# Attention with one exponential per key tile for both heads, scores issued ahead of the value matmuls, and a second input buffer in the first LayerNorm stage

## The chip, the cores and the metric

The kernel runs on the eight NeuronCores of one Trainium2 chip. Each core gets 4 of the 32 sequences of 2048 rows and 1024 features and runs the same program on them; the cores exchange nothing. The time is device microseconds (us) of the slowest core. Each core has TensorE (PE, with its weight loads shown apart as PEld), VectorE (DVE), ScalarE (ACT), GpSimd (POOL) and SyncE (SP); every engine works through its own instructions in order and waits on semaphores. On-chip memory is SBUF; matmul results land in PSUM.

## The reference

```python
xn = layernorm(x)                       # over the 1024 features, eps 1e-5
x  = x + attn(xn) + ffn(xn)
# attn: 16 heads. q1, q2, k1, k2 = xn @ W (4 numbers per head each)
L_q = exterior(q1, q2); L_k = exterior(k1, k2)      # 6 numbers, normalised
scores = einsum(L_q, L_k @ J6.T) * 6 ** -0.5        # causal mask, softmax
out = einsum(softmax(scores), xn @ W_v.T + b_v) @ W_out.T + b_out
# ffn: complex linear map with W_real, W_imag (512x512, unfolded from small factors)
out_real = x_real @ W_real.T - x_imag @ W_imag.T + bias_real
out_imag = x_real @ W_imag.T + x_imag @ W_real.T + bias_imag
```

## The kernel before

A core works on its 4 images one after another. For each image there are these stages:

- `A1_tile` (lines 270 to 297): for one of 16 row tiles (128 rows x 1024) SP loads x into `xst`; DVE squares it into `x2st`, sums both and works out mean and variance; ACT makes the reciprocal deviation by Ln and Exp (lines 287, 289); DVE writes the normalised tile to `xnst` (line 294). `A2_tile` transposes it on PE (line 307) through the two PSUM banks F6 and F7 into `xnT`.
- `B1_chunk` and `B2_chunk` project q and k and build the six numbers per head; `V_group` (line 401) makes the values, kept in `vaug` with a column of ones for each head, so that row 64 of the product is the softmax denominator; `FFN_pass1` does the complex map and writes y.
- Attention: for each of 4 groups `g` of four heads, `C_scatter` spreads the six numbers of the heads over partitions (32 a head), then 8 calls of `C_pair`: `pr` (which 2 of the 4 heads) times `w` (which 512 queries). All heads' outputs go to `oT`; `burst_outproj` multiplies by `W_out` and adds to y by DMA.

`C_pair(b, g, pr, w)` is where most of the time goes, with 128 calls in a run. It walks over `nkt = 4 * w + 4` key tiles `kt` of 128 keys; there are 1280 such steps in a run. The last four steps of a call lie on the causal diagonal; they work on 512, 384, 256 and 128 queries and need a triangular mask on their first 128. The other steps work on all 512. For head j of 2, a step has a score matmul (S, line 557, only 6 rows deep; the two heads use different row groups of the array), an exponential on ACT (line 578) from PSUM `S` to `exps`, on the diagonal a mask on DVE (line 583), and a value matmul (AV, line 591) that adds into `O4`. `S` and `exps` have two slots, used by even and odd `kt`. S runs two steps ahead: `emit_scores(0)` and `emit_scores(1)` stand at the start, `emit_scores(kt + 2)` behind the AV matmuls of `kt`.

The division by the softmax sum is put off: `emit_divide` of one call (lines 610 to 639) is issued in the next, after its first two S steps. ACT takes Ln and Exp of the sum row (lines 618, 620), SP sends the result to DRAM (625) and reads it back to 64 partitions (630), and DVE multiplies (636) from `O4` to `oT`. Since there is a single `O4`, the first AV of the next call waits until that is done (`o4_free`).

Work of the next image's stages is woven into attention: `pace()` at the end of each step issues items of two queues (`A1_tile`, `A2_tile`, `FFN_pass1`, and from the fourth group on `B1_chunk`, `B2_chunk`, `V_group`). In the last image there is none of it. In the first image stages A, B, V and FFN come ahead of attention with nothing beside them; its A stage also has the 16 steps that unfold the FFN weights, two behind each of tiles 0 to 7.

Below, AV(k), S(k), exp(k) and mask(k) are those of step `kt` = k of a call, and n is its number of steps. A pair is one call of `C_pair`.

Of the kernel before, what the change touches and what calls it, by code (L numbers as in the profile page):

```python
# [9 lines left out]
F32 = mybir.dt.float32  # L10
BF16 = mybir.dt.bfloat16
AF = mybir.ActivationFunctionType
OP = mybir.AluOpType
AX = mybir.AxisListType
# [74 lines left out]
def mkap(sl, extra_offset, free_dims, nparts=None):  # L89
    p = list(sl.ap[0])  # L90
    if nparts is not None:
        p[1] = nparts
    return AP(sl.tensor, sl.offset + extra_offset, [p] + [list(d) for d in free_dims])


def pi_out_ap(tens):
    return mkap(tens, 0, [[512, 2], [1, 32], [32, 16]])


def build(nb=NB, debug=False):  # L100
# [4 lines left out]
    x_d = din("x", [nb, T, D])  # L105
# [23 lines left out]
    with st:  # L129
# [12 lines left out]
        tri_sb = sb("tri", [128, 128], BF16)  # L142
# [12 lines left out]
        exp_sb = sb("exps", [128, 2048], BF16)  # L155
        xstage = sb("xst", [128, 1024], F32)
# [14 lines left out]
        for name in ["dwp", "dxp", "dws", "dyt", "dx", "dx2", "dyp", "dya", "dbo", "dbi", "dtr", "t", "v", "s"]:  # L171
# [6 lines left out]
        TE, VE, SE, GE, SY = nc.tensor, nc.vector, nc.scalar, nc.gpsimd, nc.sync  # L178

        stx = {  # L180
            "xst_r": 0,
            "x2_r": 0,
            "xn_r": 0,
            "f_w": [0, 0],
# [82 lines left out]
        unf_steps = deque([(lambda ri=ri, mt=mt: unf_step(ri, mt))  # L267
                           for ri in range(2) for mt in range(8)] + [unf_fin])

        def A1_tile(b1, tt):  # L270
            vS.wait(SY, stx["xst_r"])
            dx.inc(SY.dma_start(xstage[:], x_d[b1, tt * 128:(tt + 1) * 128, :]), 16)
            dx.wait(VE)
            dx2.wait(VE)
            vS.inc(VE.tensor_tensor(x2stage[:], xstage[:], xstage[:], OP.mult))
            vS.inc(VE.reduce_sum(stat[:, 0:1], xstage[:], axis=AX.X))
            vS.wait(VE)
            vS.inc(VE.reduce_sum(stat[:, 1:2], x2stage[:], axis=AX.X))
            stx["x2_r"] = vS.n
            vS.inc(VE.tensor_scalar(stat[:, 2:3], stat[:, 0:1], 1.0 / 1024, None, OP.mult))  # L280
            vS.wait(VE)
            vS.inc(VE.tensor_scalar(stat[:, 3:4], stat[:, 1:2], 1.0 / 1024, None, OP.mult))
            vS.inc(VE.tensor_tensor(stat[:, 4:5], stat[:, 2:3], stat[:, 2:3], OP.mult))
            vS.wait(VE)
            var_s = vS.inc(VE.tensor_tensor(stat[:, 5:6], stat[:, 3:4], stat[:, 4:5], OP.subtract))  # L285
            vS.wait(SE, var_s)
            sS.inc(SE.activation(stat[:, 6:7], stat[:, 5:6], AF.Ln, bias=cvec[:, 0:1]))  # L287
            sS.wait(SE)
            rstd_s = sS.inc(SE.activation(stat[:, 7:8], stat[:, 6:7], AF.Exp, scale=cvec[:, 2:3]))
            sS.wait(VE, rstd_s)  # L290
            vS.wait(VE)
            tS.wait(VE, stx.get("xn_r", 0))
            dx2.wait(VE)
            xn_s = vS.inc(VE.tensor_scalar(pi_out_ap(xnstage[:]), xstage[:], stat[:, 2:3],  # L294
                                           stat[:, 7:8], OP.subtract, OP.mult))
            stx["xst_r"] = xn_s
            stx["a_xn"] = xn_s

        def A2_tile(b1, tt):
# [238 lines left out]
                                       S_ps[:, pset * 1024:pset * 1024 + 512]))  # L538

        def C_pair(b, g, pr, w, pace=None):  # L540
            last_kt = 4 * w + 3
            nkt = 4 * w + 4
            exp_snap = {}
# [23 lines left out]
            if stx.get("pending_div") is not None:  # L567
                stx["pending_div"]()
                stx["pending_div"] = None
            avj = {}  # L570
            for kt in range(nkt):
                off = max(kt * 128 - w * 512, 0)
                ss = kt % 2
                for j in range(2):
                    base = ss * 1024 + j * 512 + off
                    end = ss * 1024 + (j + 1) * 512
                    tS.wait(SE, max(avj.get((kt - 2, j), av_snap.get(kt - 2, 0)), sc_snap[kt]))
                    sS.inc(SE.activation(exp_sb[:, base:end], S_ps[:, base:end], AF.Exp))  # L578
                    ej = sS.n
                    if kt >= 4 * w:  # L580
                        sS.wait(VE, ej)
                        in0 = exp_sb[:, base: base + 128]
                        mk = vS.inc(VE.tensor_tensor(in0, in0, tri_sb[:, 0:128], OP.mult))  # L583
                        vS.wait(TE, mk)
                    else:
                        sS.wait(TE, ej)
                    if kt == 0 and j == 0:
                        vS.wait(TE, stx["o4_free"])
                    m4 = 2 * pr + j
                    h = 4 * g + m4  # L590
                    tS.inc(TE.matmul(  # L591
                        O4[:, j * 512 + off:(j + 1) * 512],
                        vaug[:, kt * 1040 + h * 65: kt * 1040 + h * 65 + 65],
                        exp_sb[:, base:end],
                        start=(kt == 0), stop=(kt == last_kt)))
                    avj[(kt, j)] = tS.n
                exp_snap[kt] = sS.n
                av_snap[kt] = tS.n
                if kt + 2 < nkt:
                    emit_scores(kt + 2)  # L600
                if pace is not None:
                    pace()
            stx["av_prev"] = [av_snap[nkt - 2], av_snap[nkt - 1]]
# [39 lines left out]
            stx["pending_div"] = emit_divide  # L643

        for tt in range(NT):
            A1_tile(0, tt)
            A2_tile(0, tt)
            for _ in range(2):
                if unf_steps:
                    unf_steps.popleft()()  # L650
# [94 lines left out]
```

How the kernel before makes its waits and increments, by code:

```python
    def inc(self, instr, k=1):  # L81
        instr.then_inc(self.h, k)
        self.n += k
        return self.n
    def wait(self, eng, n=None):
        eng.wait_ge(self.h, self.n if n is None else n)
```

## Time and profile before

| what | value |
|---|---|
| median of 2 runs | 4822.6 us (4808.25 to 4836.95) |
| the profiled execution | 4833.0 us |
| its span on the slowest core (core 5) | 4831.9 us |
| spans of the eight cores | 4792.6 to 4831.9 us |
| PE busy | 2923.8 us, 61% of the span |
| ACT busy | 1553.7 us, 32% |
| DVE busy | 1447.1 us, 30% |
| first image's stages A, B, V, FFN | 0 to about 560 us |
| attention of the last image | about 4010 to 4720 us |

The busy shares are means over stages of different kinds. The granted clock of PE is a share of 2.4 GHz: 0.50 is 1.2 GHz and 1.00 is 2.4 GHz.

### The profile page before, as it was taken

The numbers are of one execution on the slowest core, as the hardware profiler recorded it, in microseconds if no ns is written. First come the engines' busy times: TensorE is split into PE (matmuls) and PEld (weight loads), VectorE is DVE, ScalarE is ACT, GpSimd is POOL, SyncE is SP. The second block draws the span as 40 slices with busy tenths as digits, with TensorE's granted clock in tenths as the row PEclk, the third lists the DMA queues.
The fourth block names the chain that finished last, engine by engine and source line by source line (L and its number), as shares of the span: only waits on it lengthen the run. The fifth ranks groups of instructions, "written<-read, shape, count | busy, mean of one in ns | idle before, by whom it ended". The sixth has DMA issues, their size and how long they took to land.

```text
span 4831.9 us, 41653 instructions; the slowest of 8 cores (4792.6 to 4831.9 us)
## 1 busy us (share of the span) xinstructions
PE 2923.8 (61%) x10528; PEld 1013.5 (21%) x10528; DVE 1447.1 (30%) x3345; ACT 1553.7 (32%) x3009; POOL 139.4 (3%) x210
## 2 busy tenths in 40 slices
PE   2257555566656755566655865556665586666665
PEld 1114111122112411112211421112221151111112
DVE  4524334332223234332222333433222231111111
ACT  0000244443331044443433014444342204555550
POOL 1200000000000000000000000000000000000001
PEclk9959655566657955556665865556665695555558
DMA  4502201011100410112100041011110032000004
GB/s 107 47 0 70 83 27 33 27 62 61 44 9 7 60 36 27 33 31 66 62 27 11 9 69 33 27 33 48 61 57 7 5 44 35 14 12 12 14 11 72
DMA packets 87180, 180.62 MB, mean 37 GB/s; under 512 B 41760, under 2 KB 42920, under 8 KB 86960
## 3 DMA queue, kind: packets, MB, share of 16 engines
q0 software_dynamic: 56672, 75.38, 8.3%
q1 hardware_dynamic: 30288, 102.58, 7.3%
q8 instruction: 105, 1.72, 0.1%
q14 instruction: 115, 0.94, 0.1%
HBM read 114.36 MB, written 69.73 MB: 38 GB/s over the span
## 4 chain that ended last, share of the span: by engine, by line
PE 46%; DMA 22%; DVE 14%; ACT 10%; issue 8%; DVEq 1%; SPq 0%; ACTq 0%; POOLq 0%; POOL 0%
PE O L591 18%; DMA cdiv<-rscr 10%; PE S L557 8%; DMA y<-ost 8%; PE F L401 5%; PE F L437 3%; DVE oT L636 3%; DMA rscr<-cdiv 3%; ACT cdiv L620 3%; ACT exps L578 3%; ACT cdiv L618 3%; PE F L444 2%; PE F L327 2%; DVE exps L583 1%; PE F L384 1%
## 5 line engine op out<-in xcount | busy, mean ns | idle before, releaser
L578 ACT ACTIVATE exps<-S 128x512 bf16<-128x512 f32 (+3 forms) x2560 | 1199.0, 531 | 2117.9 <-PE S L557 2085.4
L591 PE MATMUL O<-exps,vaug 128*65 128x512 bf16 (+3 forms) x2560 | 1098.0, 511 | 1270.6 <-DVE oT L636 764.3
L591 PEld LDWEIGHTS O<-exps,vaug 128*65 128x65 bf16 x2560 | 281.5, 132 | 1797.2 <-issue 1754.4
L557 PE MATMUL S<-fqp,fkp 6*128 6x512 bf16 (+3 forms) x2560 | 625.1, 501 | 6.2 <-DVE fkp L537 5.5
L636 DVE TENSOR_TENSOR oT<-O,cdiv 64x512 bf16<-64x512 f32 x256 | 174.8, 683 | 905.3 <-DMA cdiv<-rscr 901.2
L583 DVE TENSOR_TENSOR exps<-exps,tri 128x128 bf16<-128x128 bf16 x1024 | 202.6, 225 | 718.5 <-ACT exps L578 712.0
L506 PE MATMUL S<-wout,oT 128*128 128x512 bf16 x1024 | 259.2, 415 | 93.7 <-DVE ost L515 84.2
L557 PEld LDWEIGHTS S<-fqp,fkp 6*128 6x128 bf16 x2560 | 132.8, 97 | 682.1 <-issue 663.1
L401 PE MATMUL F<-wv,xnT 128*128 128x256 bf16 x2048 | 244.2, 276 | 0.6 <-DVE vaug L413 0.5
L307 PE MATMUL F<-idt,xnst 128*128 128x128 f32 x512 | 124.8, 425 | 161.0 <-DVE xnst L294 160.9
L401 PEld LDWEIGHTS F<-wv,xnT 128*128 128x128 bf16 x2048 | 186.5, 98 | 63.4 <-issue 30.4
L377 ACT ACTIVATE scr<-F,cvec 16x512 f32<-16x512 f32 x32 | 21.6, 675 | 491.9 <-PE F L375 491.9
L618 ACT ACTIVATE cdiv<-O 1x1024 f32<-1x1024 f32 x128 | 130.2, 1017 | 128.8 <-PE O L591 128.8
L515 DVE COPY ost<-S 128x1024 f32<-128x1024 f32 x64 | 78.4, 1225 | 293.2 <-DMA y<-ost 250.0
L506 PEld LDWEIGHTS S<-wout,oT 128*128 128x128 bf16 x1024 | 104.3, 105 | 247.0 <-issue 166.3
L620 ACT ACTIVATE cdiv<-cdiv,cvec 1x1024 f32<-1x1024 f32 x128 | 146.8, 1147 | 11.8
L411 DVE TENSOR_TENSOR vaug<-F,bvbc 128x256 bf16<-128x256 f32 x256 | 109.4, 427 | 127.9 <-PE F L401 127.7
L312 DVE CAST xnT<-F 128x512 bf16<-128x512 f32 x128 | 88.6, 692 | 188.3 <-PE F L307 188.3
L452 DVE TENSOR_TENSOR ost<-F,ballbc 128x512 f32<-128x512 f32 x64 | 44.3, 692 | 333.7 <-PE F L437 333.7
L287 ACT ACTIVATE stat<-stat,cvec 128x1 f32<-128x1 f32 x64 | 18.9, 295 | 377.0 <-DVE stat L285 376.7
L307 PEld LDWEIGHTS F<-idt,xnst 128*128 128x128 f32 x512 | 100.4, 223 | 182.2 <-issue 179.8
L437 PE MATMUL F<-wr,xnT 128*128 128x512 bf16 x256 | 100.8, 537 | 48.2 <-DVE negscr L428 48.0
(72 smaller groups left out, 1964.4 us busy)
## 6 DMA issues: line engine op xcount, KB each, us to landing
y<-ost POOLq DMA_DIRECT2D x128, 512.0 KB, 5.3
xst<-x SPq DMA_DIRECT2D x64, 512.0 KB, 4.4
x2st<-x SPq DMA_DIRECT2D x64, 512.0 KB, 4.3
cdiv<-rscr SPq DMA_DIRECT2D x128, 256.0 KB, 3.7
wv<-wvT POOLq DMA_DIRECT2D x8, 256.0 KB, 20.7
wout<-woutT POOLq DMA_DIRECT2D x8, 256.0 KB, 21.5
tascr<-qk POOLq DMA_DIRECT2D x16, 128.0 KB, 2.0
rscr<-cdiv SPq DMA_DIRECT2D x128, 4.0 KB
```

Source lines behind the costliest of these rows:

```text
L307: tS.inc(TE.transpose(Fb[:, c4 * 128:(c4 + 1) * 128], xnstage[:, c * 128:(c + 1) * 128], idt_sb[:]))
L401: ins = TE.matmul(Fb[:, 0:256], xnT[:, kc * 2048 + tt * 128: kc * 2048 + tt * 128 + 128], wv_sb[:, kc * 1024 + g * 256: kc * 1024 + g * 25 ...
L411: vS.inc(VE.tensor_tensor(vaug_ap, Fb[:, 0:256], bvs, OP.add))
L437: ins = TE.matmul(F6[:, 0:512], lhsT, rhs, start=(kc == 0), stop=(kc == 7))
L506: ins = TE.matmul(Pp[:, half * 512:half * 512 + 512], oT[:, pt * 2048 + tt * 128: pt * 2048 + tt * 128 + 128], wout_sb[:, pt * 1024 + half ...
L557: tS.inc(TE.matmul(S_ps[:, ss * 1024 + j * 512 + soff: ss * 1024 + j * 512 + 512], fk_pad[32 * m4:32 * m4 + 6, kt * 128:kt * 128 + 128], f ...
L578: sS.inc(SE.activation(exp_sb[:, base:end], S_ps[:, base:end], AF.Exp))
L583: mk = vS.inc(VE.tensor_tensor(in0, in0, tri_sb[:, 0:128], OP.mult))
L591: tS.inc(TE.matmul(O4[:, j * 512 + off:(j + 1) * 512], vaug[:, kt * 1040 + h * 65: kt * 1040 + h * 65 + 65], exp_sb[:, base:end], start=(k ...
L618: sS.inc(SE.activation(cdiv[32:33, 0:1024], O4[64:65, 0:1024], AF.Ln))
L620: r_s = sS.inc(SE.activation(cdiv[0:1, 0:1024], cdiv[32:33, 0:1024], AF.Exp, scale=cvec[0:1, 3:4]))
L636: vS.inc(VE.tensor_tensor(oT[rr:rr + 64, pt * 2048 + w * 512: pt * 2048 + w * 512 + 512], O4[0:64, j * 512:j * 512 + 512], cdiv[0:64, j * ...
```

## The change

Two edits. In the first image's A stage, odd tiles are loaded into the space of `exps` (not yet in use) with a semaphore of their own, so that two loads can be under way; later images keep one buffer. In `C_pair`, exp and mask of the two heads become one instruction each (of 1024 elements, or 2 x 384, 2 x 256, 2 x 128; the mask of 2 x 128), the AV matmuls of a step come in a row behind them, and `emit_scores(kt + 2)` moves from behind the AV matmuls of `kt` to ahead of them, behind exp(kt). One wait of ACT, on the last use of the `exps` space as input buffer, is added ahead of the first exp.

```diff
--- before.py
+++ after.py
@@ -178,7 +178,7 @@
         TE, VE, SE, GE, SY = nc.tensor, nc.vector, nc.scalar, nc.gpsimd, nc.sync
 
         stx = {
-            "xst_r": 0,
+            "xst_rs": [0, 0],
             "x2_r": 0,
             "xn_r": 0,
             "f_w": [0, 0],
@@ -267,13 +267,16 @@
         unf_steps = deque([(lambda ri=ri, mt=mt: unf_step(ri, mt))
                            for ri in range(2) for mt in range(8)] + [unf_fin])
 
-        def A1_tile(b1, tt):
-            vS.wait(SY, stx["xst_r"])
-            dx.inc(SY.dma_start(xstage[:], x_d[b1, tt * 128:(tt + 1) * 128, :]), 16)
-            dx.wait(VE)
-            dx2.wait(VE)
-            vS.inc(VE.tensor_tensor(x2stage[:], xstage[:], xstage[:], OP.mult))
-            vS.inc(VE.reduce_sum(stat[:, 0:1], xstage[:], axis=AX.X))
+        def A1_tile(b1, tt, slot=0):
+            xs = xstage[:] if slot == 0 else exp_sb[:, 0:2048].bitcast(F32)
+            dxs = dx if slot == 0 else dx2
+            vS.wait(SY, stx["xst_rs"][slot])
+            dxs.inc(SY.dma_start(xs, x_d[b1, tt * 128:(tt + 1) * 128, :]), 16)
+            dxs.wait(VE)
+            if slot == 0:
+                dx2.wait(VE)
+            vS.inc(VE.tensor_tensor(x2stage[:], xs, xs, OP.mult))
+            vS.inc(VE.reduce_sum(stat[:, 0:1], xs, axis=AX.X))
             vS.wait(VE)
             vS.inc(VE.reduce_sum(stat[:, 1:2], x2stage[:], axis=AX.X))
             stx["x2_r"] = vS.n
@@ -291,9 +294,9 @@
             vS.wait(VE)
             tS.wait(VE, stx.get("xn_r", 0))
             dx2.wait(VE)
-            xn_s = vS.inc(VE.tensor_scalar(pi_out_ap(xnstage[:]), xstage[:], stat[:, 2:3],
+            xn_s = vS.inc(VE.tensor_scalar(pi_out_ap(xnstage[:]), xs, stat[:, 2:3],
                                            stat[:, 7:8], OP.subtract, OP.mult))
-            stx["xst_r"] = xn_s
+            stx["xst_rs"][slot] = xn_s
             stx["a_xn"] = xn_s
 
         def A2_tile(b1, tt):
@@ -538,6 +541,9 @@
                                        S_ps[:, pset * 1024:pset * 1024 + 512]))
 
         def C_pair(b, g, pr, w, pace=None):
+            if not stx.get("xbuf_ok"):
+                vS.wait(SE, stx["xst_rs"][1])
+                stx["xbuf_ok"] = True
             last_kt = 4 * w + 3
             nkt = 4 * w + 4
             exp_snap = {}
@@ -567,37 +573,40 @@
             if stx.get("pending_div") is not None:
                 stx["pending_div"]()
                 stx["pending_div"] = None
-            avj = {}
             for kt in range(nkt):
                 off = max(kt * 128 - w * 512, 0)
                 ss = kt % 2
+                tS.wait(SE, max(av_snap[kt - 2], sc_snap[kt]))
+                if off:
+                    e_out = mkap(exp_sb[:], ss * 1024 + off, [[512, 2], [1, 512 - off]])
+                    e_in = mkap(S_ps[:], ss * 1024 + off, [[512, 2], [1, 512 - off]])
+                else:
+                    e_out = exp_sb[:, ss * 1024: ss * 1024 + 1024]
+                    e_in = S_ps[:, ss * 1024: ss * 1024 + 1024]
+                sS.inc(SE.activation(e_out, e_in, AF.Exp))
+                exp_snap[kt] = sS.n
+                if kt + 2 < nkt:
+                    emit_scores(kt + 2)
+                if kt >= 4 * w:
+                    sS.wait(VE, exp_snap[kt])
+                    in0 = mkap(exp_sb[:], ss * 1024 + off, [[512, 2], [1, 128]])
+                    tri_b = mkap(tri_sb[:], 0, [[0, 2], [1, 128]])
+                    mk = vS.inc(VE.tensor_tensor(in0, in0, tri_b, OP.mult))
+                    vS.wait(TE, mk)
+                elif kt + 2 >= nkt:
+                    sS.wait(TE, exp_snap[kt])
+                if kt == 0:
+                    vS.wait(TE, stx["o4_free"])
                 for j in range(2):
-                    base = ss * 1024 + j * 512 + off
-                    end = ss * 1024 + (j + 1) * 512
-                    tS.wait(SE, max(avj.get((kt - 2, j), av_snap.get(kt - 2, 0)), sc_snap[kt]))
-                    sS.inc(SE.activation(exp_sb[:, base:end], S_ps[:, base:end], AF.Exp))
-                    ej = sS.n
-                    if kt >= 4 * w:
-                        sS.wait(VE, ej)
-                        in0 = exp_sb[:, base: base + 128]
-                        mk = vS.inc(VE.tensor_tensor(in0, in0, tri_sb[:, 0:128], OP.mult))
-                        vS.wait(TE, mk)
-                    else:
-                        sS.wait(TE, ej)
-                    if kt == 0 and j == 0:
-                        vS.wait(TE, stx["o4_free"])
                     m4 = 2 * pr + j
                     h = 4 * g + m4
-                    tS.inc(TE.matmul(
+                    ins = TE.matmul(
                         O4[:, j * 512 + off:(j + 1) * 512],
                         vaug[:, kt * 1040 + h * 65: kt * 1040 + h * 65 + 65],
-                        exp_sb[:, base:end],
-                        start=(kt == 0), stop=(kt == last_kt)))
-                    avj[(kt, j)] = tS.n
-                exp_snap[kt] = sS.n
+                        exp_sb[:, ss * 1024 + j * 512 + off: ss * 1024 + (j + 1) * 512],
+                        start=(kt == 0), stop=(kt == last_kt))
+                tS.inc(ins)
                 av_snap[kt] = tS.n
-                if kt + 2 < nkt:
-                    emit_scores(kt + 2)
                 if pace is not None:
                     pace()
             stx["av_prev"] = [av_snap[nkt - 2], av_snap[nkt - 1]]
@@ -643,7 +652,7 @@
             stx["pending_div"] = emit_divide
 
         for tt in range(NT):
-            A1_tile(0, tt)
+            A1_tile(0, tt, tt % 2)
             A2_tile(0, tt)
             for _ in range(2):
                 if unf_steps:
```

On PE, at the start of the very last pair (w = 3 of the last image; the pair before it ends with AV of 128 columns). L557 and L591 are S and AV. Before:

```order
L591 MATMUL O<-exps,vaug 65x128 [waits sem_v] x2
L557 MATMUL S<-fqp,fkp 128x512 [waits sem_s,sem_v]
L557 MATMUL S<-fqp,fkp 128x512
L557 MATMUL S<-fqp,fkp 128x512 [waits sem_s,sem_v]
L557 MATMUL S<-fqp,fkp 128x512
L591 MATMUL O<-exps,vaug 65x512 [waits sem_s,sem_v]
L591 MATMUL O<-exps,vaug 65x512 [waits sem_s]
L557 MATMUL S<-fqp,fkp 128x512 [waits sem_s]
L557 MATMUL S<-fqp,fkp 128x512
L591 MATMUL O<-exps,vaug 65x512 [waits sem_s] x2
```

In the changed kernel, where S is L563 and AV is L603:

```order
L603 MATMUL O<-exps,vaug 65x128 [waits sem_v]
L603 MATMUL O<-exps,vaug 65x128
L563 MATMUL S<-fqp,fkp 128x512 [waits sem_s,sem_v]
L563 MATMUL S<-fqp,fkp 128x512
L563 MATMUL S<-fqp,fkp 128x512 [waits sem_s,sem_v]
L563 MATMUL S<-fqp,fkp 128x512
L563 MATMUL S<-fqp,fkp 128x512 [waits sem_s]
L563 MATMUL S<-fqp,fkp 128x512
L603 MATMUL O<-exps,vaug 65x512 [waits sem_v]
L603 MATMUL O<-exps,vaug 65x512
L563 MATMUL S<-fqp,fkp 128x512 [waits sem_s]
L563 MATMUL S<-fqp,fkp 128x512
```

S(2), which stood behind AV(0), now stands ahead of it, and so ahead of the wait for `o4_free` (sem_v). From then on each S(k+2) waits for exp(k) before AV(k); the AV of undisturbed steps carry no wait of their own.

On PE at the end of the same pair, before:

```order
L557 MATMUL S<-fqp,fkp 128x384 [waits sem_s]
L557 MATMUL S<-fqp,fkp 128x384
L591 MATMUL O<-exps,vaug 65x512 [waits sem_v] x2
L557 MATMUL S<-fqp,fkp 128x256 [waits sem_s]
L557 MATMUL S<-fqp,fkp 128x256
L591 MATMUL O<-exps,vaug 65x384 [waits sem_v] x2
L557 MATMUL S<-fqp,fkp 128x128 [waits sem_s]
L557 MATMUL S<-fqp,fkp 128x128
L591 MATMUL O<-exps,vaug 65x256 [waits sem_v] x2
L591 MATMUL O<-exps,vaug 65x128 [waits sem_v] x2
```

and now:

```order
L563 MATMUL S<-fqp,fkp 128x256 [waits sem_s]
L563 MATMUL S<-fqp,fkp 128x256
L603 MATMUL O<-exps,vaug 65x512 [waits sem_v]
L603 MATMUL O<-exps,vaug 65x512
L563 MATMUL S<-fqp,fkp 128x128 [waits sem_s]
L563 MATMUL S<-fqp,fkp 128x128
L603 MATMUL O<-exps,vaug 65x384 [waits sem_v]
L603 MATMUL O<-exps,vaug 65x384
L603 MATMUL O<-exps,vaug 65x256 [waits sem_v]
L603 MATMUL O<-exps,vaug 65x256
L603 MATMUL O<-exps,vaug 65x128 [waits sem_v]
L603 MATMUL O<-exps,vaug 65x128
```

The last three AV steps now follow each other with only their masks (sem_v) between them.

## Rows read from the trace of the kernel before

**Rows 1.** The page's chain that ended last, by engine.
```profile
PE 46%; DMA 22%; DVE 14%; ACT 10%; issue 8%; DVEq 1%; SPq 0%; ACTq 0%; POOLq 0%; POOL 0%
```
**Rows 2.** Waits of the run: engine line <- releaser: us in total, times, longest.
```profile
DVE oT L636 <- DMA cdiv<-rscr: 901.2, 128, 9.1
PE O L591 <- DVE oT L636: 764.3, 96, 9.1
PE O L591 <- DVE exps L583: 456.2, 238, 9.5
```
**Rows 3.** Timeline, last image, an undisturbed stretch: start us, us, engine, line, operation.
```profile
4142.60 0.61 PE L557 MATMUL S<-fqp,fkp 6*128 6x512 bf16 x2
4143.14 1.06 PE L591 MATMUL O<-exps,vaug 128*65 128x512 bf16 x2
4143.33 1.08 ACT L578 ACTIVATE exps<-S 128x512 bf16<-128x512 f32 x2 [0.45 <-PE S L557]
...
4144.13 0.61 PE L557 MATMUL S<-fqp,fkp 6*128 6x512 bf16 x2
```
**Rows 4.** Windows: PE, PEld, DVE, ACT, POOL busy, PEclk, DMA share, GB/s.
```profile
4144.00:4148.00 4.00, 4.00 (x12) 0.87 (x12) 0.00 (x0) 2.65 (x6) 0.00 (x0) 0.50 0.00 0
...
816.00:818.00 2.00, 1.89 (x10) 0.62 (x8) 0.00 (x0) 2.00 (x5) 0.00 (x0) 1.00 0.00 0
```
**Rows 5.** Timeline, last image: end of one pair, start of the next.
```profile
4152.02 0.85 PE L591 MATMUL O<-exps,vaug 128*65 128x384 bf16 x2
...
4153.07 0.67 PE L591 MATMUL O<-exps,vaug 128*65 128x256 bf16 x2
4153.21 0.45 ACT L578 ACTIVATE exps<-S 128x128 bf16<-128x128 f32 x2 [0.34 <-PE S L557]
4153.59 0.39 DVE L583 TENSOR_TENSOR exps<-exps,tri 128x128 bf16<-128x128 bf16 x2 [0.39 <-ACT exps L578]
...
4153.96 0.46 PE L591 MATMUL O<-exps,vaug 128*65 128x128 bf16 x2 [0.23 <-DVE exps L583]
...
4154.57 1.02 ACT L618 ACTIVATE cdiv<-O 1x1024 f32<-1x1024 f32 x1 [0.91 <-PE O L591]
...
4156.85 2.06 ACT L578 ACTIVATE exps<-S 128x512 bf16<-128x512 f32 x4
...
4162.15 1.40 DVE L636 TENSOR_TENSOR oT<-O,cdiv 64x512 bf16<-64x512 f32 x2 [8.16 <-DMA cdiv<-rscr]
...
4163.69 1.04 PE L591 MATMUL O<-exps,vaug 128*65 128x512 bf16 x2 [8.29 <-DVE oT L636]
```
**Rows 6.** Timeline, first image, a stretch at the full clock.
```profile
815.17 0.62 PE L591 MATMUL O<-exps,vaug 128*65 128x512 bf16 x2
815.36 5.19 ACT L578 ACTIVATE exps<-S 128x512 bf16<-128x512 f32 x10 [1.56 <-PE S L557]
...
815.72 0.39 PE L557 MATMUL S<-fqp,fkp 6*128 6x512 bf16 x2
...
816.11 0.86 PE L591 MATMUL O<-exps,vaug 128*65 128x512 bf16 x2
```
**Rows 7.** Groups by form: busy us, mean ns | idle before, releaser.
```profile
L578 ACT ACTIVATE exps<-S 128x512 bf16<-128x512 f32 x1792 | 954.4, 595 | 1711.7 <-PE S L557 1705.2
L557 PE MATMUL S<-fqp,fkp 6*128 6x512 bf16 x1792 | 489.5, 562 | 4.4 <-DVE fkp L537 3.8
L583 DVE TENSOR_TENSOR exps<-exps,tri 128x128 bf16<-128x128 bf16 x1024 | 202.6, 225 | 718.5 <-ACT exps L578 712.0
L578 ACT ACTIVATE exps<-S 128x128 bf16<-128x128 f32 x256 | 56.9, 273 | 209.3 <-PE S L557 183.5 <-PE O L591 25.1
```
**Rows 8.** Line 275 in the first 230 us: idle ahead of it, us, times.
```profile
  DMA xst<-x: 16.0, 10
```
**Rows 9.** Chain, first 240 us: start us, us, what.
```profile
11.18 13.04 DMA xst<-x
...
32.39 8.56 DMA xst<-x
```

## The prediction

> **What bounds the kernel now.** First the chain that ended last: PE has 46% of it, DMA 22%, DVE 14%, ACT 10% [rows 1]. No engine is full, so the waits come next. The largest sits at the start of a pair: DVE waits 901.2 us, in all 128 pairs, for the read-back of the divisor; PE waits 764.3 us for DVE's multiplication in the 96 pairs with w of 1 or more. For w = 0 the same wait ends with a mask and stands among the 456.2 us under line 583 [rows 2]. Third, the timeline of a pair in the last image, where nothing is woven in. PE starts S, 0.54 us later AV, 0.99 us later S again: 1.53 us a step with no gap, while ACT needs 1.08 us and idles 0.45 us [rows 3]. So an undisturbed step is bound by PE. The clock is at 0.50 (1.2 GHz) there though PE is busy in all of the 4 us; in the first image, behind woven-in matmuls, there are stretches at 1.00 (2.4 GHz), and there ACT is the full engine, 2.00 of 2.00 us [rows 4], at 5.19 us for ten exps, 1.04 us a step [rows 6].
>
> The reader is to see three regions: a gap of 8.3 us between pairs, set by ACT, two DMAs and DVE [rows 5]; cold steps set by PE; warm steps set by ACT. The change has to be priced in each.
>
> **Lags, read once.** AV ends 0.07 us after the next matmul starts (1.06 against 0.99, 0.61 against 0.54) [rows 3]. From the end of AV to ACT's next start: 4153.96 + 0.46 to 4154.57, 0.15 us. From exp to mask: 4153.21 + 0.27 to 4153.59, 0.11 us. From mask to AV: 4153.59 + 0.22 to 4153.96, 0.15 us [rows 5]. From exp to PE: 815.36 + 0.60 to 816.11, 0.15 us [rows 6].
>
> **The merged exp.** 512 columns take 595 ns, 128 take 273 [rows 7]: 0.84 ns a column. So 1024 columns are 1.02 us, 768 are 0.81, 512 are 0.60, 256 are 0.38. The 1x1024 Ln took 1.02 us [rows 5], which agrees. Bounds: 0.86 (columns alone) and 1.19 (two single ones). I take 1.02. **The merged mask** has no row: 0.22 us (one of 128 columns) and 0.45 (two) bound it; I take 0.39, what a pair takes now [rows 5, 7].
>
> **The undisturbed step, cold.** PE's own work stays 1.53 us. New is a ring: exp(k), then S(k+2), then AV(k), then exp(k+2), since AV(k) now stands behind S(k+2) and exp(k+2) needs both. It is 1.02 + 0.15 + 0.54 + 1.06 + 0.15 = 2.92 us for two steps, 1.46 a step. That is just under 1.53, so PE still binds and the step costs nothing; the cover is 0.15 us in two steps. ACT's saving of some 0.06 us a step lies in its 0.45 us of idle time and is worth nothing. Ends: with the exp at 1.19 the ring has 3.09 us, 0.01 over; there are 768 steps without a mask (24 for each of 32 groups of four pairs), so this end is +6 us.
>
> Does the AV lose its exposed weight load, now that it has no wait of its own? S starts 0.54 us before AV where 512 columns at 1.2 GHz are 0.43: 0.11 us are exposed [rows 3]. The Trainium skill (TensorE: Matmul & The Clock Gate, "Packing small matmuls — row/col tiling") says that a weight load overlaps matmuls in flight only when the row group differs. By that rule nothing is hidden, as AV takes all rows and S sits in two of them, and the sum stays; without it PE's step would be 1.42 us. Rows 3 agree as far as they go: AV's exp had been ready well before.
>
> **The undisturbed step, warm.** PE has 0.55 us for AV (815.17 to 815.72) and 0.32 for S (0.39 less 0.07) [rows 6]. Ring: 1.02 + 0.15 + 0.32 + 0.62 + 0.15 = 2.26, 1.13 us a step against 1.04 now. Before, the ring was cut shorter, as AV of head 0 ran beside exp of head 1. So a warm step is 0.09 us slower. How many are warm: 1792 S matmuls of 512 columns took 489.5 us [rows 7], 0.55 us a step; cold ones show 0.61, warm ones 0.39 [rows 3, 6], so at most 29% are warm, less because S(0) and S(1) run close behind each other. I take a quarter, 192 of 768: **+17 us** (0 to +20; with the exp at 0.86, +2).
>
> **The start of a pair.** S(2) moves into the 8.3 us gap [rows 5]: exp(0) ends about 1.0 us after 4156.85, AV(0) starts at 4163.69. Nothing late comes of it: SP's two DMAs and DVE's multiplication don't wait for PE here. That takes 0.54 us off PE behind the gap. exp(2) then starts when AV(0) ends and is done 1.17 us later; PE has S(3) and AV(1) meanwhile, 1.53 us.
>
> **The end of a pair, where some of it is given back.** Up to AV(n-4) PE now has done S(n-2) too, 256 columns, 0.54 - 0.21 = 0.33 us. From the end of AV(n-4)'s slot, before: S(n-2) 0.33, then the rows from 4152.02 to 4154.42, 2.73 us in all [rows 5]. Now: exp(n-2) starts at 0.22, ends at 0.82, its mask at 1.32, AV(n-2) starts at 1.47. PE was free at 1.00 (S(n-1) 0.22, AV(n-3) 0.78), so it idles 0.47 us. AV(n-2) has 0.60, to 2.07. exp(n-1) starts at 1.22, when AV(n-3) has ended, ends at 1.60, its mask at 2.10, AV(n-1) runs 2.25 to 2.71. So the end takes the same 2.7 us with 0.33 us less to do in it: it became bound by the chain of exp and mask. Net 0.54 - 0.33 + 0.02 = 0.23 us for each of 96 pairs: **-22 us** (0 to -52: with masks at 0.45 and later semaphores nothing is left; with a free end it is all 0.54).
>
> **Pairs with w = 0** have nothing but such an end: 2.7 us behind AV(0) in both. AV(0) itself waits for one mask of 0.39 in place of the first of two, 0.17 us: 32 x 0.17 = **+5 us** (-5 to +8).
>
> **The first A stage.** DVE waited 16.0 us for x in ten of 16 tiles [rows 8]. The first wait, 1.7 us of it, stays, as nothing precedes it. The others go: a load issued a tile ahead has that tile's whole time. **-14 us.** What is late next is DVE's own row of instructions. The second load now runs beside the weight loads, where the first took 13.04 us against 8.56 for the second [rows 9]; it has until about 37 us. If it delays the first load, 3 us come back (-11 to -16). One more wait of ACT, ahead of the first exp, is satisfied by then. Woven-in A1 tiles keep one buffer and their place on SP.
>
> **Sum.** 4833.0 - 14 - 22 + 5 + 17 = 4819 us, 14 less than the profiled execution. That execution is 10.4 us above the median shown, so the median goes from 4822.6 to about 4809. A measurement of this kernel can tell about 2% from no change; this is 0.3%.
>
> **Rivals.**
> 1. Slower: the merged exp closes the ring. If an ACTIVATE over two PSUM banks costs 1.5 us, the ring has 3.40 us, 1.70 a step: 0.17 x 576 cold steps = 98, and 0.24 x 192 = 46 more in the warm ones: 4809 + 144 = 4953. It decides from 1.17 us on. Against it: the Ln of 1024 columns spans two banks in 1.02 us [rows 5]. Chance 0.07.
> 2. The clock rises. If the new order lets cold stretches run at 2.4 GHz, 576 steps go from 1.53 to 1.13 us: -230, 4579 us. For it: PE is at half clock for whole stretches in which it never rests [rows 4], so something small may decide. Against it: columns and order within a step hardly change. The Trainium skill (the same page, "The HAM clock gate") says that sustained activity releases the throttle; rows 4 don't bear that out for this mix. Chance 0.12.
> 3. The clock falls: the warm stretches are lost, 192 x (1.53 - 1.04) = 94 less the 17 counted: 4886. For it: PE now rests inside warm steps. Chance 0.05.
> 4. The AV weight load is hidden. PE's step is 1.42, the ring's 1.46 binds: -0.07 x 576 = -40, 4769 us. Chance 0.10.
> 5. The end of a pair costs nothing more, all 0.54 us stay: 96 x 0.31 = -30, 4779 us. Chance 0.10.
>
> **Numbers.** The forecast has chance 0.56, 4809 us. Faster by over 2% (below 4726) is rival 2 and a little of 4 and 5 together: 0.13. Slower by over 2% (above 4919) is rival 1 and a little of 3: 0.08. Within 2%: 0.79. The range 4735 to 4875 takes in the forecast's bounds and rivals 4 and 5, and leaves out 1, 2 and 3.
>
> **What would show it.** Merged exp of 1024 near 1.02 us. In the last image a step still of 1.53 us with ACT idle about 0.5; at full clock 1.13 us a step and ACT no longer full. S of 512 columns inside the gap. Idle ahead of AV under the mask line grown: about 0.47 us at AV(n-2) in each pair. No wait for DMA at the x2st line but the first. Clock of cores near 0.64. I am wrong if the step in the last image isn't 1.53 us, if the exp is over 1.17 us, or if the mean clock moves by over 0.02.

## The result, and the profile after

The changed kernel takes 4735.9 us (median of 11 runs) against 4820.1 us (10 runs): ratio 0.982, 95% interval 0.980 to 0.984, 84 us less. I had forecast 14 us less. All spans of the profiled executions fell, by 96 us in the mean of the eight cores (die medians 4797 and 4820 us, now 4706 and 4710); the mean granted clock of the cores was 0.639 to 0.655 and is 0.651 to 0.662. The profiled core is core 1, span 4743.7 us.

The waits of the changed kernel, which answer to [rows 2] (S is L563, exp L586, mask L594, AV L603, division L645):

```profile
DVE oT L645 <- DMA cdiv<-rscr: 922.2, 128, 9.7
PE O L603 <- DVE oT L645: 506.2, 96, 6.5
PE S L563 <- ACT exps L586: 417.3, 237, 7.1
PE O L603 <- DVE exps L594: 307.2, 269, 6.4
```

The wait for the division, 764.3 us before, is now two waits, since S(2) stands in the middle of it. The chain behind it is as long as it was. The idle time of PE is therefore nearly unchanged in sum (249 and 238 us in the attention of the last image, 1322 and 1320 us in the woven images, means of eight cores); what changed is that 0.54 us of work in each gap no longer has to be done later.

An undisturbed step of the last image, which answers to [rows 3]:

```profile
4044.25 0.61 PE L563 MATMUL S<-fqp,fkp 6*128 6x512 bf16 x2
4044.41 1.02 ACT L586 ACTIVATE exps<-S 128x1024 bf16<-128x1024 f32 x1 [6.07 <-PE O L603]
...
4044.79 1.06 PE L603 MATMUL O<-exps,vaug 128*65 128x512 bf16 x2
...
4045.78 0.61 PE L563 MATMUL S<-fqp,fkp 6*128 6x512 bf16 x2
...
4045.95 1.02 ACT L586 ACTIVATE exps<-S 128x1024 bf16<-128x1024 f32 x1 [0.51 <-PE O L603]
```

From S to S it is 1.53 us as before; the exp takes 1.02 us and ACT idles 0.51. A step at the full clock, which answers to [rows 6]:

```profile
1282.97 0.62 PE L603 MATMUL O<-exps,vaug 128*65 128x512 bf16 x2
1283.57 0.39 PE L563 MATMUL S<-fqp,fkp 6*128 6x512 bf16 x2
1283.69 1.94 ACT L586 ACTIVATE exps<-S 128x1024 bf16<-128x1024 f32 x2 [0.27 <-PE O L603]
1283.89 0.62 PE L603 MATMUL O<-exps,vaug 128*65 128x512 bf16 x2
1284.86 0.39 PE L563 MATMUL S<-fqp,fkp 6*128 6x512 bf16 x2 [0.35 <-ACT exps L586]
1285.18 0.62 PE L603 MATMUL O<-exps,vaug 128*65 128x512 bf16 x2
1285.78 0.39 PE L563 MATMUL S<-fqp,fkp 6*128 6x512 bf16 x2
```

Two steps take 2.21 us (1283.57 to 1285.78). Now both engines rest: ACT 0.27 us for AV, PE 0.35 us for the exp. That is the ring. Over all cores, two undisturbed full-clock steps in a row take 1.10 us each in the median, and 1.03 before. The end of one pair and the start of the next, which answer to [rows 5]:

```profile
4050.06 0.29 PE L563 MATMUL S<-fqp,fkp 6*128 6x128 bf16 x2
...
4050.28 0.85 PE L603 MATMUL O<-exps,vaug 128*65 128x384 bf16 x2
4050.93 0.29 DVE L594 TENSOR_TENSOR exps<-exps,tri 128x256 bf16<-128x256 bf16 x1 [0.81 <-ACT exps L586]
4051.23 0.38 ACT L586 ACTIVATE exps<-S 128x256 bf16<-128x256 f32 x1 [0.40 <-PE O L603]
...
4051.36 0.61 PE L603 MATMUL O<-exps,vaug 128*65 128x256 bf16 x2 [0.23 <-DVE exps L594]
4051.72 0.29 DVE L594 TENSOR_TENSOR exps<-exps,tri 128x256 bf16<-128x256 bf16 x1 [0.49 <-ACT exps L586]
...
4052.15 0.39 PE L603 MATMUL O<-exps,vaug 128*65 128x128 bf16 x2 [0.18 <-DVE exps L594]
...
4056.15 0.61 PE L563 MATMUL S<-fqp,fkp 6*128 6x512 bf16 x2 [2.63 <-ACT exps L586]
...
4061.57 1.03 PE L603 MATMUL O<-exps,vaug 128*65 128x512 bf16 x2 [4.82 <-DVE oT L645]
```

S(2) lies in the gap, at 4056.15. The merged mask takes 0.29 us. exp(n-1) (4051.23) starts when AV(n-3) has ended (4050.28 + 0.85), before AV(n-2) starts; so the chain that sets the end is exp(n-1), mask(n-1), AV(n-1), and one mask stands in it. From the end of AV(n-4)'s slot (4050.06) to the end of AV(n-1) (4052.54) it is 2.48 us. In the first stage, the line that answers to [rows 8] shows one wait for x, the first:

```profile
  DMA xst<-x: 1.6, 1
```

To compare kernels region by region I took, for each of the 128 pairs and all eight cores, the time from the start of the first AV to the end of the last, in one profiled execution of each kernel. Means in us, by w; "woven" are images 0 to 2:

```
                            last image, w = 0 1 2 3      woven, w = 0 1 2 3
before                       3.78  9.72 15.93 22.01    11.16 15.28 25.73 27.27
changed                      3.49  9.27 15.40 21.58    10.76 14.46 24.54 26.98
merge alone                  3.80 10.19 16.31 22.40    11.36 15.46 25.97 27.95
order alone                  3.26  8.98 15.15 21.24    10.48 14.00 23.46 25.40
order, joint waits           3.58  9.47 15.61 21.83    10.97 14.76 25.50 27.34
order, one mask              3.34  9.16 15.37 21.42    10.70 14.22 23.75 25.58
only S(2) ahead              3.32  8.96 14.92 21.01    10.82 14.55 24.17 26.26
all ahead but S(2)           3.47  9.41 15.57 21.67    10.82 14.55 24.86 25.76
```

Each column stands for 8 pairs of the last image, or 24 woven ones. For the changed kernel that gives 8 x 1.70 = 14 us in the last image and 24 x 2.70 = 65 us in the others; to the first AV it is 16 us less (medians 551.9 and 535.8). That is 95 us, where the mean span of the cores fell by 96; the medians of all runs differ by 84.

A second execution of either kind says how far the table can be trusted. The kernel with the buffer alone has the attention of before; its woven columns are 0.04 to 0.19 us lower, 10 us in sum. The kernel of both without the buffer has the changed attention; its woven columns give 24 x 2.44 = 59 us in place of 65. The gain in the woven images is thus known to about 10 us. The time to the first AV is 547.0 to 551.9 us in the eight kernels without the buffer and 535.8 to 541.6 in the six with it.

### The profile page after: what moved, and what is told of

Same layout as the page of the kernel before. It is cut to its first block, busy times and chain, and to the rows that moved or that the text cites. A ratio compares the mean times of both kernels' runs of the same rounds, so it can differ in the third digit from the quotient of the medians.

```text
span 4743.7 us, 36014 instructions; the slowest of 8 cores (4685.8 to 4743.7 us)
## 1 busy us (share of the span) xinstructions
PE 2852.9 (60%) x10528; PEld 978.1 (21%) x10528; DVE 1385.7 (29%) x2833; ACT 1475.2 (31%) x1729; POOL 139.9 (3%) x210
## 4 chain that ended last, share of the span: by engine, by line
PE 44%; DMA 22%; DVE 14%; ACT 12%; issue 7%; DVEq 0%; SPq 0%; ACTq 0%; POOLq 0%; POOL 0%
PE O L603 18%; DMA cdiv<-rscr 10%; DMA y<-ost 8%; PE S L563 7%; PE F L404 5%; ACT exps L586 4%; PE F L440 3%; DVE oT L645 3%; DMA rscr<-cdiv 3%; ACT cdiv L629 3%; ACT cdiv L627 3%; PE F L447 2%; PE F L330 2%; DVE exps L594 1%; PE F L310 1%
## 5 line engine op out<-in xcount | busy, mean ns | idle before, releaser
L586 ACT ACTIVATE exps<-S 128x1024 bf16<-128x1024 f32 (+3 forms) x1280 | 1120.6, 893 | 2099.8 <-PE O L603 1366.1
L603 PE MATMUL O<-exps,vaug 128*65 128x512 bf16 (+3 forms) x2560 | 1052.2, 512 | 845.4 <-DVE oT L645 506.2
L563 PE MATMUL S<-fqp,fkp 6*128 6x512 bf16 (+3 forms) x2560 | 626.1, 498 | 423.8 <-ACT exps L586 417.3
L603 PEld LDWEIGHTS O<-exps,vaug 128*65 128x65 bf16 x2560 | 232.5, 137 | 1293.2 <-issue 1274.0
L645 DVE TENSOR_TENSOR oT<-O,cdiv 64x512 bf16<-64x512 f32 x256 | 174.9, 683 | 926.3 <-DMA cdiv<-rscr 922.2
L563 PEld LDWEIGHTS S<-fqp,fkp 6*128 6x128 bf16 x2560 | 141.1, 97 | 1152.8 <-issue 1146.9
L594 DVE TENSOR_TENSOR exps<-exps,tri 128x256 bf16<-128x256 bf16 x512 | 143.3, 291 | 746.4 <-ACT exps L586 743.8
```

Source lines behind the costliest of these rows:

```text
L563: tS.inc(TE.matmul(S_ps[:, ss * 1024 + j * 512 + soff: ss * 1024 + j * 512 + 512], fk_pad[32 * m4:32 * m4 + 6, kt * 128:kt * 128 + 128], f ...
L586: sS.inc(SE.activation(e_out, e_in, AF.Exp))
L594: mk = vS.inc(VE.tensor_tensor(in0, in0, tri_b, OP.mult))
L603: ins = TE.matmul(O4[:, j * 512 + off:(j + 1) * 512], vaug[:, kt * 1040 + h * 65: kt * 1040 + h * 65 + 65], exp_sb[:, ss * 1024 + j * 512 ...
L645: vS.inc(VE.tensor_tensor(oT[rr:rr + 64, pt * 2048 + w * 512: pt * 2048 + w * 512 + 512], O4[0:64, j * 512:j * 512 + 512], cdiv[0:64, j * ...
```

## The experiments

Each ran together with the kernel before on one chip; "less" and "more" are against the median of its runs there (4816.6 to 4824.0 us). Ratios carry their 95% interval. In the cuts of code, "..." marks lines left out.

**The buffer alone** (the first part of the diff, C_pair as before).

> The kernel before with only the second input buffer of the first A stage. Before as 4820 us. Theory 1 (the buffer is worth the waits for x it removes, as predicted): 14 us less, ratio 0.997; idle for DMA ahead of the x2st line 1.6 us in place of 16.0, first value matmul 14 to 16 us earlier, attention unchanged. Theory 2 (the freed time is lost to a later stage or to contention with the weight loads): 0 to 5 us less, ratio 0.999 to 1.000. Rest of the gain of 85 us must then lie in attention by either.

4807.2 us, 0.998 (0.9965 to 0.9993), 12 us less; first AV 12 us earlier. Theory 1 holds, a little under its size.

**The order alone.** Both exps come first, then S(k+2), then mask and AV of each head, each of them with a wait of its own as before.

```diff
                     sS.inc(SE.activation(exp_sb[:, base:end], S_ps[:, base:end], AF.Exp))
-                    ej = sS.n
+                    ejs.append(sS.n)
+                exp_snap[kt] = sS.n
+                if kt + 2 < nkt:
+                    emit_scores(kt + 2)
+                for j in range(2):
...
-                        sS.wait(VE, ej)
+                        sS.wait(VE, ejs[j])
...
-                        sS.wait(TE, ej)
+                        sS.wait(TE, ejs[j])
...
-                if kt + 2 < nkt:
-                    emit_scores(kt + 2)
```

> The kernel before with S(k+2) issued ahead of AV(k), exps and masks still one for each head, no second buffer. Theory 1 (the order carries the attention's gain, since S(2) of 0.54 us runs in the gap between pairs): 40 to 50 us less, ratio 0.990 to 0.992; the cold step stays 1.53 us, a full-clock step goes from 1.02 to about 1.1. Theory 2 (merging carries it, the order alone gives its gain back at the end of a pair, as the prediction worked out): 0 to 20 us less, ratio 0.996 to 1.000.

4653.9 us, 0.966 (0.9645 to 0.968): 165 us less, twice what the whole change gains and far over both theories. So the merging, or what came with it, must cost.

**The merge alone** (exp and mask as in the change, `emit_scores` behind AV).

> The kernel before with merged exp and merged mask, S(k+2) still behind AV(k), no second buffer. Theory 1 (order carries the gain): 5 to 15 us less, ratio 0.997 to 0.999, as the merged mask takes 0.29 us in place of 0.39 at the end of each pair. Theory 2 (merging carries it): 40 to 60 us less, ratio 0.988 to 0.992. A third outcome, slower than before (ratio over 1.002), would say that the split of the two heads had hidden latency, at full clock above all, and that the order pays for it.

4876.4 us, 1.014 (1.011 to 1.016): the third outcome, 58 us more.

**Both, without the buffer.**

> The changed kernel without the second input buffer. If the parts add up, the gain is that of the changed kernel less that of the buffer alone: 85 - 15 = 70 us less than before, ratio 0.985 to 0.986. Theory 1: equal to the sum of order alone and merge alone within 10 us. Theory 2 (the two need each other): 20 us or more beyond that sum.

4760.8 us, 0.988 (0.986 to 0.990), 58 us less. The sum of the parts is -165 + 58 = -107, so neither theory's rule fits: together they are 49 us worse than their sum. Merging costs more where S is ahead. The buffer is the difference to the changed kernel, 84 - 58 = 26 us, twice what it gave alone, though the first AV is only 11 us earlier; the two intervals just overlap, so its size is not known better than some 10 to 20 us.

**The changed kernel with two masks.**

```diff
-                    mk = vS.inc(VE.tensor_tensor(in0, in0, tri_b, OP.mult))
+                    for j in range(2):
+                        in0 = exp_sb[:, ss * 1024 + j * 512 + off: ss * 1024 + j * 512 + off + 128]
+                        mk = vS.inc(VE.tensor_tensor(in0, in0, tri_sb[:, 0:128], OP.mult))
```

> The changed kernel (exp merged, S ahead, second buffer) with the mask of each head by itself again; AV still waits for both. Order alone made 4654 us, order with merged exp and mask 4761, so merging costs about 107 us there. Theory E (the merged exp costs it: a longer ring at full clock, exp(k+2) of head 0 no longer starting after AV(k) of head 0): as the changed kernel, 4736 us, or up to 15 us more, for the pair of masks takes 0.39 us against 0.29. Theory K (the merged mask costs it, as AV of head 0 waits for head 1): about 4660 us.

4778.0 us, 0.992 (0.9905 to 0.993). Theory K falls, and the 15 us that theory E allows are passed too: given the joint wait, one mask is some 40 us better than two. At the end of a pair this shows what one mask is worth. Its pair of masks takes 0.36 us:

```profile
4053.59 0.61 PE L603 MATMUL O<-exps,vaug 128*65 128x256 bf16 x2 [0.30 <-DVE exps L594]
4053.87 0.36 DVE L594 TENSOR_TENSOR exps<-exps,tri 128x128 bf16<-128x128 bf16 x2 [0.43 <-ACT exps L586]
...
4054.38 0.39 PE L603 MATMUL O<-exps,vaug 128*65 128x128 bf16 x2 [0.18 <-DVE exps L594]
```

From S(n-1) to the end of AV(n-1) it takes 2.57 us (mean of the last image, all cores) where the changed kernel takes 2.49. By the measure of the table, two masks cost 3 us in the last image and 18 in the woven ones.

**Order with one mask, exps apart.**

> S ahead, exps apart, but one mask for both heads, and AV of head 0 waits for exps of both. No second buffer. Theory E (merged exp costs): close to order alone, 4655 to 4680 us. Theory K (merged mask, or AV of head 0 waiting for head 1, costs): 4720 us or more, near the 4761 of both.

4697.7 us, 0.976 (0.974 to 0.978), outside the ranges of both theories, between the two kernels: 44 us over order alone. Here AV of head 0 waits for head 1, but exp of head 0 still starts behind AV of head 0.

**Only S(2) ahead, and all but S(2) ahead.**

> The kernel before with S(2) alone moved ahead of AV(0), all later S behind AV as before; exps and masks apart, no second buffer. Order alone gained 165 us. Theory G (the gap between pairs carries it: S(2) costs nothing there): 96 x 0.54 + 32 x 0.33 = 62 us at least, 4755 us, and the rest is due to the end of a pair. Theory C (a steady lead of the scores at full clock and behind woven-in work carries it): under 40 us, 4780 us or more.

4707.4 us, 0.977 (0.976 to 0.9785), 109 us less.

> The complement: every S(k+2) ahead of AV(k) but S(2), which stays behind AV(0), so nothing more is done in the gap. Theory G: little, 4790 to 4820 us. Theory C: most of the 165 us, 4690 us or less. Theory T (the end of the pair: with S(n-1) done early, exp of the last steps starts when AV of head 0 has ended): 128 pairs by 0.3 us, 4780 us.

4736.0 us, 0.983 (0.982 to 0.985), 81 us less, outside the ranges of G, C and T. G's bound of 62 us is met and passed by S(2); T gives the size of the rest in the last image, where the complement gains 0.31 to 0.36 us a pair (table): 42 us for all 128 pairs, where T had 40. Both add up to 190, and together they make 165. In the woven images each gains more than its mechanism explains, and what the rest is was not tried.

A part of the row "only S(2) ahead" is the clock. On the eight cores 16 of its 256 last-image pairs ran at a mean clock of over 0.6, with nothing woven in; in the kernel before and in the changed one none did. Its pairs that stayed at 0.50 take 3.32, 9.04, 15.26 and 21.33 us.

**Order alone with joint waits.** Every instruction keeps its size; the waits are those of the merged form, and the two AV matmuls of a step signal once. The cuts are set against the kernel with the order alone.

```diff
-                    tS.wait(SE, max(avj.get((kt - 2, j), av_snap.get(kt - 2, 0)), sc_snap[kt]))
+                tS.wait(SE, max(av_snap[kt - 2], sc_snap[kt]))
...
-                        sS.wait(VE, ejs[j])
+                    sS.wait(VE, exp_snap[kt])
...
-                        vS.wait(TE, mk)
-                    else:
-                        sS.wait(TE, ejs[j])
...
+                    vS.wait(TE, mk)
+                else:
+                    sS.wait(TE, exp_snap[kt])
```

> Order alone (4654 us, every instruction of its size: 512 columns, masks of 128) but with the waits of the merged form: exps of a step wait for AV of both heads, masks wait for both exps, AV waits for both. No second buffer. Theory W (what merging costs, 107 us, is the joint waiting; one large ACTIVATE is no dearer than two): 4760 us or more, as the merged kernel without the buffer (4761). Theory I (the merged instructions themselves cost): near 4654 us. By the ring, a full-clock step needs 1.11 + 0.15 + 0.32 + 0.62 + 0.15 = 2.35 us for two, 1.17 a step, so W expects 1.15 to 1.2 there, 1.06 for I.

4825.5 us, 1.000 (0.998 to 1.002). Theory W holds, and more: the joint waits alone cost 171 us, all that the order gains (166 us when each kernel is set against the runs of the kernel before that went with it). The merged instructions then give back 64 us (59 so counted; 4825 to 4761). Two full-clock steps in a row take 1.13 us each in the median, against 1.03 with the order alone; the ring had 1.17. Of the 138 us that the woven images take longer than with the order alone, PE is idle for 76 and busy for 62 (means of eight cores); the same matmuls run longer, and I did not separate how much of that is the clock. The end of a pair shows it: here with joint waits, PE rests 0.36 and 0.18 us,

```profile
4089.42 0.45 ACT L577 ACTIVATE exps<-S 128x128 bf16<-128x128 f32 x2 [0.34 <-PE O L595]
4089.69 0.61 PE L595 MATMUL O<-exps,vaug 128*65 128x256 bf16 x2 [0.36 <-DVE exps L586]
4089.97 0.36 DVE L586 TENSOR_TENSOR exps<-exps,tri 128x128 bf16<-128x128 bf16 x2 [0.43 <-ACT exps L577]
...
4090.48 0.39 PE L595 MATMUL O<-exps,vaug 128*65 128x128 bf16 x2 [0.18 <-DVE exps L586]
```

and in the kernel with the order alone the last six AV matmuls run in one piece, because exp of head 0 starts while AV of head 1 is running:

```profile
3963.84 0.29 PE L557 MATMUL S<-fqp,fkp 6*128 6x128 bf16 x2
...
3964.06 1.99 PE L598 MATMUL O<-exps,vaug 128*65 128x384 bf16 x6
...
3964.69 0.60 ACT L579 ACTIVATE exps<-S 128x128 bf16<-128x128 f32 x2 [0.30 <-PE O L598]
```

That is 2.21 us behind AV(n-4) against 2.48 in the changed kernel. At the full clock, right behind a woven-in item, ACT starts 0.82 us behind S and then does ten exps in a row, where the changed kernel's ACT starts 1.04 us behind S (1280.45 to 1281.49) and rests 0.27 us for AV after two.

```profile
1259.15 0.39 PE L557 MATMUL S<-fqp,fkp 6*128 6x512 bf16 x2
...
1259.97 5.19 ACT L579 ACTIVATE exps<-S 128x512 bf16<-128x512 f32 x10 [5.36 <-PE O L598]
```

**Order and buffer**, the change without its merging.

> S ahead of AV and the second input buffer, exps and masks apart: the change without its merging. If the parts add up: 4654 us of order alone less 10 to 15 of the buffer, 4640 us, ratio 0.963. If the buffer's gain is lost in company, 4655 us.

4663.2 us, 0.967 (0.965 to 0.968). No faster than order alone (0.966): the first AV is 7 us earlier in the profiled executions (547.6 and 540.3), and the woven images, where the two kernels are the same, take 17 us longer. A difference of that size between executions hides the buffer here.

**S ahead at the two ends of a pair only.**

> S ahead of AV only at step 0 (in the gap) and in the four diagonal steps (end of a pair), behind AV in between; exps and masks apart, second buffer. At full clock the steps between should take 1.02 us as before the change, in place of 1.06. If the gain sits at the two ends and the lead in between only costs: 5 to 20 us under the kernel with S ahead everywhere, 4620 to 4635 us. If the lead in between is worth something by itself behind woven-in work: 4650 us or more.

4678.5 us, 0.971 (0.969 to 0.9735), slower than S ahead throughout. The second outcome holds. The last image gained 8 us (885 against 894 from Ln to Ln, means of eight cores), but more than half of that is the clock: here too 16 of the 256 pairs of the last image ran at over 0.6, and those that stayed at 0.50 gained 0.15 us at most. The woven images lost 3 to 8 us each. The lead in between is worth something behind woven-in work.

**The gap itself.** The kernel of order and buffer, with O4 emptied at once. The multiplication follows in step min(nkt - 1, 5) of the next pair; the undivided result is rounded to bf16 in between, once more than before.

```diff
+                tS.wait(VE, max(av_last, stx["ot_r"]))
+                for j in range(2):
...
+                    vS.inc(VE.tensor_copy(o_ap, O4[0:64, j * 512:j * 512 + 512]))
+                cp = vS.n
...
+                stx["o4_free"] = cp
+                stx["o4_free_s"] = ln_s
...
+                    dbi.wait(VE, bin_s)
+                    vS.wait(VE, cp)
+                    for o_ap, j in outs:
+                        cd = cdiv[0:64, j * 512:j * 512 + 512]
+                        vS.inc(VE.tensor_tensor(o_ap, o_ap, cd, OP.mult))
```

> As the one above, and the gap between pairs attacked: DVE copies the undivided result from O4 to oT at once (1.4 us), ACT takes Ln of the sum row, and then O4 is free; the multiplication by the divisor follows some steps later, in place. So AV(0) of the next pair no longer waits for the two DMAs. Theory G (the gap bounds the kernel, 9.4 us in each of 128 pairs): the gap falls to about 3 us, set by Ln, Exp and exp(0) in a row on ACT, less 2.7 us where a pair with w = 0 is too short for the DMAs: 128 x 6.4 - 86 = 730 us less, 3910 us; below that if the clock rises with less idle time. Rival (the chain of the divisor moves to the next place, or DVE is blocked by the late multiplication): less than 400 us gained, over 4240 us.

4138.3 us, 0.859 (0.857 to 0.861): 684 us less than before, 525 less than the kernel it is built on, where theory G had 730 and the rival under 400. It is the fastest version here. The gap fell from 9.5 to 4.2 us, not 3 (to 5.0 or 5.4 behind a pair with w = 0), and the woven pairs became longer by 58 us in sum:

```profile
3701.47 2.06 ACT L585 ACTIVATE exps<-S 128x512 bf16<-128x512 f32 x4
...
3702.70 0.61 PE L563 MATMUL S<-fqp,fkp 6*128 6x512 bf16 x2 [2.51 <-ACT exps L585]
...
3703.24 1.06 PE L605 MATMUL O<-exps,vaug 128*65 128x512 bf16 x2
...
3706.63 1.40 DVE L661 TENSOR_TENSOR oT<-oT,cdiv 64x512 bf16<-64x512 bf16 x2 [6.09 <-DMA cdiv<-rscr]
```

ACT's Ln, Exp and exp(0) now set AV(0), and since the order puts S(2) ahead of AV(0), its 0.54 us are in the way here: what was free cover before is on the path now. That is read from these rows; the same kernel with S(2) behind AV(0) was not run.

## Why the prediction was wrong

- **Right.** The cold step (1.53 us, ACT idle 0.5), the exp of 1.02 us, S(2) in the gap, the gap itself, the ring at full clock (1.13 forecast; 1.11 in the rows above, 1.10 in the median of all, from 1.03), the single wait for x and -14 us for it (16 to the first AV, 12 us by the run with the buffer alone). None of the rivals happened; the mean clock moved by 0.01.
- **The start and the end of a pair**, the terms -22 and +5. I had 0.23 us for w of 1 or more and a loss of 0.17 for w = 0. The last image shows 0.45, 0.53, 0.43 and a gain of 0.29. The step that failed is the length of the end: from the end of AV(n-4)'s slot to the end of AV(n-1) it took 2.48 us in place of my 2.71. I had its shape right, the chain from exp to mask to AV(n-1), and three of its pieces too long. The merged mask, for which I took 0.39 us out of bounds of 0.22 and 0.45, takes 0.29; the kernel with two masks, where the end takes 0.08 us more, confirms its share. AV(n-1) takes 0.39 where I copied 0.46 from [rows 5]: there AV of the second head waits for a mask of its own, and now the two run in a row. And exp(n-1) starts 0.10 us behind AV(n-3), where I took a lag of 0.15. For w = 0 there was the same mask in front: from its start to AV(0) it is 0.54 us (4029.98 to 4030.52) against 0.48, so AV(0) starts 0.06 to 0.07 us later, not 0.17, and the shorter end more than pays for it. By the last image's rates over all 128 pairs that is 32 x 1.70 = 54 us where I had 17.
- **The woven images**, the term +17. They gained 24 us beyond the last image's rates (14 or 18 when the second execution of either attention is taken), though their full-clock steps did cost 0.07 us each, about 10 us for the 130 to 160 of a core that are undisturbed. The step that failed here is that I carried the price of a step from undisturbed stretches to all of them and gave woven-in work no term. Two parts are to be seen. An item that follows a full AV at half clock now leaves it a slot of 0.86 us (1347.25 to 1348.11 in the rows below), where AV in front of S has 0.99; there are some 64 such items a core (half of the transposes, the FFN items and the projections), so 8 us, an estimate from these rows. And the projection that follows took 4.91 us where it took 5.71 before; over all 72 that the traces show in one piece the median is 5.03 and was 5.62 (5.04 and 5.52 in the two kernels with the same attention), so for 12 of them 7 us. How much of the rest is clock and how much is order was not tried separately. The time at full clock doesn't tell: it was 857 and 1011 us in the two executions with the attention of before, 1014 and 856 in the two with the changed one.

```profile
1347.25 1.06 PE L603 MATMUL O<-exps,vaug 128*65 128x512 bf16 x2
1348.11 4.91 PE L330 MATMUL F<-xnT,wqk 128*128 128x512 bf16 x16
```

and of the kernel before:

```profile
1372.76 0.61 PE L557 MATMUL S<-fqp,fkp 6*128 6x512 bf16 x2
1373.30 5.71 PE L327 MATMUL F<-xnT,wqk 128*128 128x512 bf16 x16
```

- **What I did not see at all.** I priced the order and the merging as one thing, and so took their sum for small effects. The runs show two large ones of opposite sign: the order gives 165 us, joint waiting of the two heads takes some 170, larger instructions give some 60. A row for it was there: in [rows 6] ACT ran ten exps without a break while head 0 ran ahead of head 1. I named that in the ring, for full-clock steps, and did not carry it to the end of a pair or to the restart behind woven-in work. That 4735.9 us still lies inside my range of 4735 to 4875 is luck: its lower part stood for the bounds of my terms and rivals 4 and 5, which did not happen, and woven-in work had no part in it.
- **A reason of mine that doesn't hold.** I kept AV's exposed 0.11 us because AV takes all rows of the array. AV followed by a projection shows nothing exposed (0.86 us, twice 512 columns at 1.2 GHz), though both take all rows. The step stayed at 1.53 us, as forecast, but what exposes the load between S and AV is open.

## What to carry to other kernels

Moving work that waits for nothing ahead of a long wait is worth its time wherever nothing but that wait is behind it; here S(2) alone, two instructions in each of 128 pairs, gave 109 us. Merging the instructions of two independent streams also merges their waits: count what each stream's own semaphore let start early, above all in rings through two engines, and try the joint wait without the merge to see its price alone. And when a wait of 9 us stands 128 times in a profile, shorten its chain before filling it: that was worth 525 us, and once it was short, the filling work lay on the path by its rows. When a length is copied from a row, ask whether a wait is inside it that the change removes.

## What the runs showed of the hardware

In attention with nothing woven in, a stream in which PE never rests stayed at 0.50 of the clock for whole pairs in every version [rows 4], with two of four matmuls only 6 rows deep; in the kernel before and in the changed one it did so in all 256 pairs of the last image on the eight cores. A projection of 16 full matmuls raised it within itself (window 1348 to 1352 of the changed kernel, 0.66; the next at 1.00):

```profile
1348.00:1352.00 4.00, 4.00 (x14) 1.50 (x13) 0.60 (x1) 1.02 (x1) 0.00 (x0) 0.66 0.00 0
1352.00:1357.00 5.00, 3.94 (x21) 1.31 (x20) 1.85 (x6) 1.79 (x3) 0.00 (x0) 1.00 0.00 0
```

But the attention stream can do it too. In the kernel with only S(2) ahead a pair of w = 3 in the last image (core 1, from 4318) went to the full clock with nothing but S and AV on PE, and took 16.15 us where such pairs at 0.50 take 21.33:

```profile
4318.00:4322.00 4.00, 4.00 (x14) 1.04 (x12) 0.00 (x0) 2.67 (x6) 0.00 (x0) 0.62 0.00 0
4322.00:4326.00 4.00, 3.85 (x16) 1.14 (x14) 0.00 (x0) 4.00 (x9) 0.00 (x0) 1.00 0.01 2
```

16 of 256 pairs did so there, and 16 in the kernel with S ahead at the two ends. In both the steps in between have S behind AV, as in the kernel before, where none did. What decides is open. By the Trainium skill (TensorE: Matmul & The Clock Gate, "The HAM clock gate") sustained activity lifts the throttle; the projection agrees, the attention stream mostly does not.

The mask of 2 x 128 columns took 0.29 us where one of 128 takes 0.22: the second 128 columns cost 0.07 us, where a second instruction of its own costs 0.14 to 0.17 (pairs of masks take 0.36 or 0.39 us). The Trainium skill (VectorE: DVE Perf Modes, "The perf-mode tier table (the rule you actually need)") gives tensor_tensor on bf16 twice the rate of f32. An estimate from its 1224 ns for 2048 elements is 0.08 us for 128, and 0.14 from the 2293 ns of f32; the 0.07 us agree with the first. It bears on the term that I mis-sized, and I had not weighed it.
